# Streaming 96 instead of 104 columns in three of the four node blocks of a one-hot lookup by matmul (two-layer graph network, one core)

## What is computed

```python
el = jnp.einsum('nhf,hf->nh', feat_src, attn_l)      # 6250 nodes x 8 heads
er = jnp.einsum('nhf,hf->nh', feat_dst, attn_r)
e = el[src] + er[dst]                                # 100000 edges x 8 heads
e = jnp.where(e >= 0, e, NEG_SLOPE * e)
```

## Time and profile before

| | |
|---|---|
| median of three runs | 4147.86 us (4145.99 to 4148.17) |
| span of the profiled execution | 4150.1 us |
| TensorE, busy share of the span | 84% |
| VectorE | 55% |
| ScalarE | 43% |
| GpSimd | 63% |
| the lookup loop, first to last matmul of L1621 | 207.5 to 570.3 us |
| matmuls of L1621, of 15160 | 7536 |
| granted TensorE clock, mean | 0.956 |

### The profile page before, as it was taken

The page is one execution under the profiler, slowest core; times in us unless marked ns, Lnnn a source line. Parts: engine busy times, 40 slices in busy tenths (PEclk is TensorE's granted clock), DMA queues, the critical chain, the costliest instruction groups (busy, mean ns, idle before and its releaser), DMA issues.

```text
span 4150.1 us, 55488 instructions
## 1 busy us (share of the span) xinstructions
PE 3489.9 (84%) x15160; PEld 1694.2 (41%) x15160; DVE 2288.9 (55%) x3880; ACT 1798.3 (43%) x4172; POOL 2607.4 (63%) x2733
## 2 busy tenths in 40 slices
PE   5899988677888888898788888888997788888887
PEld 4499963222233333343333333333443333333332
DVE  6599887677777888885222333333552222333336
ACT  4356522444545555454333443444343333344442
POOL 3654411677777777654777777777106777777775
PEclk9999999899999999999999999999998999999999
DMA  7822325577777777665777777777216777777779
GB/s 285 244 67 61 90 76 208 172 210 210 210 210 211 210 210 211 190 206 190 210 210 210 210 210 210 211 210 210 79 66 211 211 210 210 210 210 210 210 209 351
DMA packets 318375, 804.24 MB, mean 194 GB/s; under 512 B 72905, under 2 KB 98139, under 8 KB 317129
## 3 DMA queue, kind: packets, MB, share of 16 engines
q0 software_dynamic: 199680, 630.72, 52.6%
q1 hardware_dynamic: 88925, 116.91, 8.5%
q10 hardware_dynamic: 29580, 54.49, 3.8%
HBM read 714.52 MB, written 88.21 MB: 193 GB/s over the span
## 4 chain that ended last, share of the span: by engine, by line
PE 34%; POOL 23%; issue 21%; DMA 12%; DVE 6%; SPq 1%; POOLq 1%; DVEq 1%; ACT 1%; ACTq 0%
POOL edge L1280 17%; PE mm L1529 8%; POOL rows_wmat L1280 5%; DMA edge<-h_tab,src_group 5%; DMA rows_wmat<-v_tab,src_group 4%; PE mm L1621 4%; PE sm L1693 4%; PE tr L1621 4%; PE mm L1693 4%; PE sm L1566 3%; PE tr L1693 2%; DVE edge L866 2%; PE tr L1524 1%; DMA ht_tab<-rows_wmat 1%; PE hist_ps L1693 1%
## 5 line engine op out<-in xcount | busy, mean ns | idle before, releaser
L1280 POOL DMA_INDIRECT edge<-h_tab,src_group x1564 | 1484.2, 949 | 708.5 <-issue 447.5
L1436 ACT ACTIVATE hots<-iota,drel 128x128 f32<-128x128 f32 x1760 | 538.0, 388 | 1174.5 <-PE tr L1693 606.9
L1280 POOL DMA_INDIRECT rows_wmat<-v_tab,src_group x782 | 739.4, 945 | 289.2 <-issue 272.4
L1693 PE MATMUL mm<-edge,hots 128*128 x880 | 465.9, 679 | 195.3 <-SPq L1098 189.7
L1693 PE MATMUL sm<-edge,hots 128*128 x880 | 442.6, 650 | 150.5 <-SPq L1098 148.1
L891 DVE TENSOR_TENSOR big<-big,mm 128x512 f32 x220 | 151.4, 688 | 686.6 <-PE tr L1693 668.8
L891 DVE TENSOR_TENSOR big<-big,sm 128x512 f32 x220 | 151.4, 688 | 602.6 <-PE misc L1693 588.6
L1693 PE MATMUL tr<-edge,hots 128*128 x880 | 395.6, 592 | 0.0
L1693 PEld LDWEIGHTS mm<-edge,hots 128*128 128x128 f32 x880 | 183.6, 217 | 470.1 <-issue 469.9
L1529 PE MATMUL mm<-rows_wmat 128*128 128x512 f32 x784 | 356.0, 598 | 0.0
L1693 PEld LDWEIGHTS sm<-edge,hots 128*128 128x128 f32 x880 | 175.8, 207 | 410.3 <-issue 410.0
(11 more groups left out here) (252 smaller groups left out, 4574.0 us busy)
## 6 DMA issues: line engine op xcount, KB each, us to landing
h_tab<-rows_wmat SPq DMA_DIRECT2D x98, 256.0 KB, 2.0
edge<-h_tab,src_group POOLq DMA_INDIRECT x1564, 3.7
rows_wmat<-low_tab SPq DMA_DIRECT2D x157, 128.0 KB
ht_tab<-rows_wmat SPq DMA_DIRECT2D x49, 256.0 KB
big<-ht_tab ACTq DMA_DIRECT2D x49, 256.0 KB, 2.8
v_tab<-rows_wmat ACTq DMA_DIRECT2D x49, 256.0 KB
x_tab<-big SPq DMA_DIRECT2D x49, 256.0 KB, 2.1
rows_wmat<-v_tab,src_group POOLq DMA_INDIRECT x782, 3.7
```

Of the source, the lines that this page charges most:

```text
L1280: pool.indirect_dma_start(ring[:, 2 * u + c, :], None, tab, bass.IndirectOffsetOnAxis(ap=src_group[:, n:n + 1], axis=0)).then_inc(a["rows_ ...
L1436: act.activation(group_hots[:, q % 2, e, :], iota[:, :], ACT.Abs, bias=drel[:, col:col + 1], scale=-1.0).then_inc(a["dist_set"], 1)
L1693: last = pe.matmul(agg_ps[bank][:, :], group_hots[:, q % 2, w % GROUP * 2 + n, :], edge[:, ds(slot[w % OFFS] + n * D, D)], start=(n == 0), ...
```

## The change

In `pick` on TensorE, the matmuls of blocks kt = 1, 2, 3 take only the 12 groups that these blocks have, 8 x 12 = 96 columns; kt = 0 stays at 8 x 13 = 104. Nothing is laid out anew: `el_parts` and the PSUM banks keep their 13 places a head. So the 96-column matmuls read 8 runs of 12 bf16 (24 bytes) with a step of 26 bytes, and write 8 runs of 12 f32 (48 bytes) with a step of 52 bytes, where both sides were one run of 104 before. The a = 12 places in PSUM get their value from the kt = 0 matmuls alone. The memset that wrote the zeros of kt = 1, 2, 3 at a = 12 is dropped.

```diff
@@ -577,7 +577,6 @@
-            did(dve.memset(el_parts[:, :, 1:, :, whole:], 0.0))
             for part, left in enumerate((eler[:, :, 0:H], el_rest, el_rest)):
@@ -1616,10 +1615,12 @@
                 for q in range(Q):
+                    sums = sum_ps[bank][:, q * NA * H:(q + 1) * NA * H].rearrange("p (h a) -> p h a", h=H)
                     for kt in range(KT):
+                        tiles = len(range(kt, TILES, KT))
                         for part in range(3):
-                            last = pe.matmul(sum_ps[bank][:, q * NA * H:(q + 1) * NA * H],
-                                             src_hot[:, par, kt, q * P:(q + 1) * P], el_parts[:, part, kt, :, :],
+                            last = pe.matmul(sums[:, :, 0:tiles], src_hot[:, par, kt, q * P:(q + 1) * P],
+                                             el_parts[:, part, kt, :, 0:tiles],
                                              start=(kt == 0 and part == 0), stop=(kt == KT - 1 and part == 2))
```

## The result

The changed kernel took 4157.32 us as median of 7 runs, the kernel before 4146.99; the ratio is 1.003 (95% interval 1.0019 to 1.0041). In runs made later the medians are 4154.73 and 4146.77 (11 and 21 runs), ratio 1.0018 (1.0009 to 1.0027). One of the seven executions of the kernel before was slow (17647.01 us), and the ratio leaves it out. The prediction was 4129.5 us, 0.44% faster: wrong in its sign. The range up to 4167 holds the time, but by its mild slower case and not by the mechanism that the forecast rested on.

What follows compares the result with a forecast made beforehand. TensorE's matmul rate was taken to bound the lookup loop: 151 groups x 0.120 = 18.1 us, plus 0.3 us at clock 0.50, made 18.4 us off 4147.9, giving 4129.5 us. The range was 4126 to 4167.

Steps and rivals of the forecast that it cites:

- mild slower case: Lookup loop's matmuls: one tick of 1.2 GHz a run break, +18 us, 4166; about a third of 0.23 at or below.
- What bounds the loop, and passes it on: Lookup loop: TensorE's matmul rate, 46.1 ns each, sets it, and all of the saving reaches the kernel's end.
- the time to "issue" at the loop's end: End of the loop: 3.97 us of TensorE waiting for code outside the loop to arrive; 2 groups' saving counted lost.
- the last group: Loop's last group of 48 matmuls, 3.92 us at clock 0.50, where the saving is double.
- The price of a column: Loop's matmuls: 0.417 ns a column, not the load of weights; 0.120 us saved of 2.213 a group.
- VectorE follows: VectorE's turn in the loop averages 2.00 us, just below TensorE's new 2.093, so it keeps up.
- The memset, covered: VectorE at 145.62: dropping 0.12 us and about 0.03 us of waiting gains 0, covered by a 12.97 us wait.
- New access pattern: The 96-column matmuls' 8 runs on read and write sides: cost taken as nothing, up to 3.1 ns kept for the range.
- Rival A, a break eats a column: Loop's 96-column matmuls: no saving, blocks stay at 4.43 us, 4144 to 4151; 0.26 shared with another rival.
- Rival B, slower: Loop's 96-column matmuls: a run break costs more than a column, +18 us (4166) or +91 us (4239); chance 0.23.
- The chances: Whole kernel: faster 0.51, same 0.26, slower 0.23.

Runs made afterwards that it cites:

- no_gaps: Kernel before with 44 of 48 matmuls of a group cut to 96 columns, one run on both sides, sums wrong; 4125.57 us beside 4149.67.
- group_major_psum: Kernel before with groups outside heads in el parts and PSUM, 96 columns in one run, VectorE reading PSUM stepped; 4130.19 us, ratio 0.9952.
- write_even: Kernel before with 44 of 48 matmuls reading one run of 96, writing 4 runs of 24, step 26, even starts; 42.7 ns a matmul.
- after: The changed kernel's first profiled execution, against the kernel before; span 4164.6 us.
- after_again: The changed kernel run once more, same program, beside runs of the kernel before; ratio 1.0018.

## Why the prediction was wrong, step by step

- *What bounds the loop, and passes it on.* Right. TensorE's pace sets it in both kernels, and the time from the loop's end to the first gather is the same within 0.3 us in the first pair of profiles (175.9 for 175.7). Two smaller terms were not settled: that the time to "issue" at the loop's end is code arriving was not shown by any run, and the last group, which the forecast took at 3.92 us, took 3.00 in the other profile of the same kernel and 2.28 in both profiles after.
- *The price of a column.* Right. 42.8 ns was worked out for 96 columns, 42.7 measured where they are one run (no_gaps). The load of weights, of which each matmul has one in both cases, sets nothing at these widths.
- *VectorE follows.* Right in what comes of it, but the margin was mis-sized. Its turn was put at 2.00 us on average; with no wait in it, it takes 2.08 (no_gaps), mostly because the three L684 take 0.97 from start to product where the earlier trace rows has 0.90. The slack at 2.093 was 0.01 us and not 0.09. group_major_psum runs at 2.09.
- *The memset, covered.* Not contradicted. It is gone from the trace, and no run measured it by itself.
- *New access pattern: this is the step that failed.* The forecast had a range for this term, nothing to 3.1 ns for eight steps, from the slower weight loads of L1650, and then took nothing because the gap is only one element. The length of the gap was the wrong thing to look at. What counts is that 13 is odd, so that every second run begins in the middle of a pair. Measured: 3.4 ns for the read side alone and 4.8 for both sides together, so the upper bound of 3.1 was too low as well. That it is close to 3.4 is luck: the row has a step at every element, and the cost turned out to hang on odd starts.
- *Rival A, a break eats a column.* Its picture (7 pairs for 6 in every second run) fits what was measured for either side alone: 45.8 ns for the write side, of which it spoke, and 46.1 for the read side. The forecast applied it to the write side only and never asked what two sides do at once. That one question is the difference between "same" and "slower": +4.8 ns for both, against the 3.3 that 8 columns give back.
- *Rival B, slower.* Its sign was right and its sizes were not: 49.5 ns or 62.8, for 47.6. Odd runs don't go at half rate, they cost about two ticks each.
- *The chances.* The row of L1650 and the arithmetic of A spoke for a cost, and against it stood, in the forecast's own words, only that nothing shows it. To give 0.51 to no cost at all was not what the rows supported.

The Trainium skill, "Advanced Engine Details and Errata", "PSUM Cachelines", says of the PSUM side that any non-contiguous pattern significantly slows matmuls and that two consecutive elements should be contiguous. The second is near what was measured. The first does not hold here: write_even, non-contiguous with even starts, takes 42.7 ns like one run.

## What to carry to other kernels

When a matmul's columns are cut out of a wider layout, look at the step of the runs on both sides, not at the size of the gap: with an even step and even starts the cut is nearly free, with an odd step each odd start costs about two columns on the side that has it (measured for bf16 read and f32 written), and when both sides have them, how they lie to each other counts too. Better still is to put the axis that is cut outermost, so that what stays is one run, and to let an engine that pays nothing for a step do the stepping, measured for that very instruction. Before an edit that speeds one engine, work out the next engine's turn; here 0.01 us of slack was just enough and 0.33 us more on one instruction was not. Take that turn from a stretch where the engine never waits, if there is one; put together from rows with waits between them it came out 0.08 us too short.

## What the runs showed of the hardware

- A matmul of 96 bf16 columns in one run, each with its own load of 128x128 weights, starts every 42.7 ns at 2.4 GHz; 104 columns every 46.1.
- 96 columns with four runs that begin on an odd element: 46.1 ns when read so, 45.8 when written so, 47.5 with eight runs of 12 on both sides whose odd ones are the same, 48.3 with four runs of 24, all odd on both sides, 46.1 with eight runs of 12 whose odd ones differ between the sides.
- 96 columns in four runs with even starts: 42.7 ns written so, 43.1 read so, 43.1 both.
- A VectorE product (128x416, f32) that reads PSUM with a step of 32 bytes takes 0.58 us, as contiguous. Its sum over the last axis of the same size takes 0.90 us instead of 0.57 when it steps 32 bytes through SBUF.
- The mean length of the gathers on GpSimd differs by 3 ns between executions of one program (945 and 948 ns for 782 of them, 948 and 951 for 1564), 6.5 us of busy time between after and after_again.
